# Cross-attention plus FFN on one core: a deeper pipeline, with probabilities and normalised rows turned by DMA transposes instead of TensorE

## The reference, cut to what matters

```python
x = x + _L0_xattn_ref(_layernorm(x, axis=-1), ctx_1024, Wq, Wk, Wv, Wskip)
x = x + _L0_ffn_ref(_layernorm(x, axis=-1), qweight, scales, zeros, bias)

def _L0_xattn_ref(pcd_up, pcd_down, Wq, Wk, Wv, Wskip):
    q = jnp.einsum('oc,bcn->bon', Wq, pcd_up)
    k = jnp.einsum('oc,bcm->bom', Wk, pcd_down)
    v = jnp.einsum('oc,bcm->bom', Wv, pcd_down)
    energy = jnp.einsum('bcn,bcm->bnm', q, k) / jnp.sqrt(C)
    attention = jax.nn.softmax(energy, axis=-1)
    x = jnp.einsum('bnm,bcm->bcn', attention, v)
    return jnp.einsum('oc,bcn->bon', Wskip, pcd_up) + x

def _L0_ffn_ref(x, qweight, scales, zeros, bias):
    w_int = nibbles of qweight, rows interleaved
    w = (w_int - jnp.round(zeros / scales).T) * scales.T
    return jnp.einsum('bsi,io->bso', x, w) + bias
```

## Time and profile before

| | us |
|---|---|
| median of 3 runs | 616.23 |
| the profiled execution, its own time | 616.67 |
| its span in the profile | 614.8 |
| PE busy | 588.1 (96%) |
| DVE busy | 476.5 (77%) |
| POOL busy | 468.7 (76%) |
| ACT busy | 409.4 (67%) |
| granted TensorE clock, mean | 0.989 |

### The profile page before, as it was taken

How to read it: one execution, slowest core, us unless ns; L and a number is a source line. 1 busy time by engine, 2 the same in 40 slices (tenths; PEclk the granted TensorE clock), 3 DMA queues, 4 the chain that set the end, 5 groups by cost and what they waited for, 6 DMA issues and landing times.

```text
span 614.8 us, 10932 instructions
## 1 busy us (share of the span) xinstructions
PE 588.1 (96%) x3348; PEld 416.1 (68%) x3348; DVE 476.5 (77%) x1027; ACT 409.4 (67%) x976; POOL 468.7 (76%) x520
## 2 busy tenths in 40 slices
PE   2868999999999999999999999999999999999996
PEld 2755777667777766777776677777677777667763
DVE  6787877878887777888778788878777877887762
ACT  4874677666668766666876666686666677666650
POOL 2453788777879877777977787897778789777866
PEclk9977999999999999999999999999999999999999
DMA  8011012222111222211222211122221112221002
GB/s 315 3 43 43 27 53 79 77 77 73 40 53 66 77 77 77 70 41 47 73 77 77 77 65 46 43 77 77 77 77 54 57 43 77 77 77 68 19 19 102
DMA packets 20178, 41.38 MB, mean 67 GB/s; under 512 B 2496, under 2 KB 7104, under 8 KB 20160
## 3 DMA queue, kind: packets, MB, share of 16 engines
q1 hardware_dynamic: 19584, 41.03, 19.7%
q10 hardware_dynamic: 576, 0.14, 0.1%
HBM read 24.39 MB, written 16.78 MB: 67 GB/s over the span
## 4 chain that ended last, share of the span: by engine, by line
PE 91%; DVE 5%; ACT 2%; issue 1%; DMA 1%; POOLq 0%; POOL 0%; ACTq 0%
PE ps_y L676 36%; PE ps_e L610 17%; PE ps_o L644 14%; PE ps_t L625 9%; PE ps_o L637 7%; PE ps_t L657 5%; PE ps_kv L688 2%; PE ps_kv L686 2%; DMA sb_x<-in_x_dram 1%; DVE sb_nib L457 1%; ACT sb_prob L288 1%; DVE sb_pt_lo L408 1%; DVE sb_neg_max L398 0%; ACT sb_pt_hi L297 0%; DVE sb_zp L499 0%
## 5 line engine op out<-in xcount | busy, mean ns | idle before, releaser
L288 ACT ACTIVATE sb_prob<-ps_e,sb_neg_max 128x256 f32<-128x256 f32 x256 | 118.7, 470 | 128.9 <-DVE sb_neg_max L398 128.8
L676 PE MATMUL ps_y<-sb_wf,sb_xnt_hi 128*128 128x512 f16 x512 | 196.1, 383 | 0.9 <-DVE sb_xnt_lo L448 0.9
L676 PE MATMUL ps_y<-sb_wf,sb_xnt_lo 128*128 128x512 f16 x512 | 194.0, 379 | 0.0
L214 POOL TENSOR_SCALAR sb_prob<-sb_prob,sb_rsum 128x256 f32<-128x256 f32 x256 | 117.7, 477 | 27.5 <-DVE sb_rsum L403 27.5
L408 DVE TENSOR_TENSOR sb_pt_lo<-ps_t,sb_pt_hi 128x512 fp32r<-128x512 f32 x128 | 88.3, 691 | 34.6 <-ACT sb_pt_hi L297 30.4
L398 DVE TENSOR_REDUCE sb_neg_max<-ps_e 128x2 f32<-128x512 f32 x128 | 87.7, 686 | 34.8 <-PE ps_e L610 34.8
L610 PE MATMUL ps_e<-sb_kv_hi,sb_xc_hi 128*128 128x256 f32 x256 | 91.6, 358 | 7.7 <-DVE sb_kv_lo L535 4.0
L297 ACT ACTIVATE sb_pt_hi<-ps_t 128x512 fp32r<-128x512 f32 x128 | 76.3, 598 | 33.9 <-PE ps_t L625 33.9
L676 PEld LDWEIGHTS ps_y<-sb_wf,sb_xnt_hi 128*128 128x128 f16 x512 | 49.7, 97 | 59.2 <-issue 17.6
L223 POOL TENSOR_TENSOR sb_rstd<-sb_ve,sb_neg_half 128x1 f32<-128x1 f32 x32 | 17.5, 548 | 92.3 <-DVE sb_ve L443 92.3
L250 POOL TENSOR_TENSOR sb_xc_lo<-sb_xc,sb_xc_hi 128x1024 fp32r<-128x1024 f32 x32 | 76.5, 2390 | 9.2 <-ACT sb_xc_hi L343 7.5
(11 more groups left out here) (85 smaller groups left out, 1162.9 us busy)
## 6 DMA issues: line engine op xcount, KB each, us to landing
sb_x<-in_x_dram SPq DMA_DIRECT2D x32, 512.0 KB, 3.3
out_dram<-sb_o SPq DMA_DIRECT2D x64, 256.0 KB, 2.1
...
sb_q<-in_L_ffn_qweight_dram SPq DMA_DIRECT2D x4, 512.0 KB, 6.4
sb_scale_row<-in_L_ffn_scales_dram SPq DMA_DIRECT2D x1, 512.0 KB, 8.7
sb_bias_row<-in_L_ffn_bias_dram SPq DMA_DIRECT2D x1, 512.0 KB, 9.5
...
```

The costliest lines, as they stand in the source:

```text
L214: last = pool.tensor_scalar(prob[:, j, t, :], prob[:, j, t, :], rsum[:, j, t:t + 1], 1.0, ALU.mult, ALU.mult)
L288: done = act.activation(prob[:, j, t, :], ps_e[j % 2][:, t, :], ACT.Exp, bias=neg_max[:, j, t:t + 1], accum_out=esum[:, j, t:t + 1])
L676: last = pe.matmul(ps_y[h][:, :], xnt_p[s][:, kt, :], wf[:, kt, h * HALF:(h + 1) * HALF], start=kt == 0 and s == 0, stop=kt == KT - 1 and ...
```

## The change

All names below are of the kernel after; its line numbers stand in the rows of instructions further down.

- **Transposes leave PE.** ACT rounds the normalised probabilities of a half (128 x 1024) to float16 `p_hi`, DVE makes the float16 rest `p_lo`, and SP issues a DMA transpose for each, SBUF to SBUF (`turn_probs`). The normalised rows are treated alike (`xn_hi` on ACT, `xn_lo` on POOL, `turn_xn`). That is 6 DMA transposes of 128 x 1024 float16 for each item, all on SP's queue, in SP's program order.
- **float16 attention.** The values are float16 in two parts too, scaled by the item's largest context entry: DVE takes it per row (`context_max`), a one-column fp32 matmul against ones sums it over rows into `ps_m`, and four small DVE instructions make the scales (`value_scale`). `residual` multiplies by `o_scale`.
- **Bias and zero point enter through PE.** One more float32r matmul of 512 columns for each FFN half (`seed_l` x `seed_row`); its left side is the row sum in two parts, brought into a row by three small DMAs. The ACT product and the two POOL sums for `rest` go; POOL adds `x1` directly.
- **One step deeper.** Attention of item `t-1`, FFN of `t-2` in step `t`, with three or four buffers for `x`, `xc`, the values, `x1`, and two for the turned rows. `ps_o` is two banks, one for each half.
- **Order.** PE in a step: scores 0, keys and values of `t+1`, attention half 0, scores 1, attention half 1, FFN half 0, scores 2, scores 3, FFN half 1.
- **No loop.** Every step is written out on every engine.
- **Start.** Wv and Wskip are scaled by DVE before they are turned; the zero-point chain is longer (`seed_sources`) and stands behind `value_scale(0)` and `stats1(1)`; `nibbles` and `unpack` are cut into other pieces.

```diff
+            def turn_probs(b, h):
+                sp.wait_ge(phi_done[h], b + 1)
+                if ran(b, 1):
+                    sp.wait_ge(attn_done[h], b)
+                sp.dma_start_transpose(pt_hi[:, h, :, :].rearrange("m k (t n) -> m (k t) n", n=P),
+                                       p_hi[:, h, :, :].rearrange("n k m -> n (k m)")).then_inc(pt_loaded[h], 16)
+                sp.wait_ge(plo_done[h], b + 1)
+                sp.dma_start_transpose(pt_lo[:, h, :, :].rearrange("m k (t n) -> m (k t) n", n=P),
+                                       p_lo[:, h, :, :].rearrange("n k m -> n (k m)")).then_inc(pt_loaded[h], 16)
+            def turn_xn(a):
+                par = a % 2
+                sp.wait_ge(xnhi_done, a + 1)
+                if ran(a, 2):
+                    sp.wait_ge(y_done[1], a - 1)
+                sp.dma_start_transpose(xnt_hi[:, par, :, :],
+                                       xn_hi[:, :, :].rearrange("c k r -> c (k r)")).then_inc(xnt_loaded[par], 16)
+                sp.wait_ge(rs3_done, a + 1)
+                if a == 0:
+                    sp.wait_ge(seed_made, 3)
+                for k, row in ((0, 0), (1, 1), (0, 32)):
+                    sp.dma_start(seed_l[row:row + 1, par, :].bitcast(F32),
+                                 rs3[:, par, k:k + 1].bitcast(F32)).then_inc(rs_loaded[par], 16)
+                sp.wait_ge(xnlo_done, a + 1)
+                sp.dma_start_transpose(xnt_lo[:, par, :, :],
+                                       xn_lo[:, :, :].rearrange("c k r -> c (k r)")).then_inc(xnt_loaded[par], 16)
...
+            def xn_low(a):
+                pool.wait_ge(xnhi_done, a + 1)
+                for k in (0, KT // 2):
+                    last = pool.tensor_tensor(xn_lo[:, k:k + KT // 2, :], xn[:, k:k + KT // 2, :],
+                                              xn_hi[:, k:k + KT // 2, :], ALU.subtract)
+                last.then_inc(xnlo_done, 1)
+
+            def step(t):
+                m, n, b, a, c = t + 2, t + 1, t, t - 1, t - 3
+                if ran(c):
+                    write_out(c, 0)
+                    write_out(c, 1)
+                if ran(b):
+                    normalise(b, 0)
+                if ran(m):
+                    inverse_std1(m)
+                if ran(n):
+                    centred_lo(n, 0)
+                if ran(b):
+                    normalise(b, 1)
+                if ran(a):
+                    inverse_std2(a)
+                if ran(n):
+                    centred_lo(n, 1)
+                if ran(a):
+                    split_row_sum(a)
+                if ran(b):
+                    normalise(b, 2)
+                    normalise(b, 3)
+                if ran(a):
...
+            def probs_hi(b, h):
+                act.wait_ge(norm_done[2 * h], b + 1)
+                act.wait_ge(norm_done[2 * h + 1], b + 1)
+                if ran(b, 1):
+                    act.wait_ge(pt_loaded[h], 32 * b)
+                act.activation(p_hi[:, h, :, :].rearrange("n k (t m) -> n k t m", m=P),
+                               prob[:, 2 * h:2 * h + 2, :, :].rearrange("n j t (k m) -> n k (j t) m", m=P),
+                               ACT.Copy).then_inc(phi_done[h], 1)
...
+            def xn_high(a):
+                act.wait_ge(xn_done, a + 1)
+                if ran(a, 1):
+                    act.wait_ge(xnt_loaded[(a - 1) % 2], nth(a - 1, 2, 32))
+                act.activation(xn_hi[:, :, :], xn[:, :, :], ACT.Copy).then_inc(xnhi_done, 1)
...
+            def step(t):
+                n, b, a = t + 1, t, t - 1
+                if ran(n):
+                    centre(n)
+                if ran(b):
+                    exps(b, 0)
+                if ran(n):
+                    keys_values_hi(n)
+                    centred_hi(n)
+                if t == -1:
+                    unpack(0)
+                if ran(b):
+                    exps(b, 1)
+                if t == 0:
+                    unpack(1)
+                if ran(b):
+                    probs_hi(b, 0)
+                if ran(a):
+                    apply_norm2(a)
+                if ran(b):
+                    exps(b, 2)
+                    exps(b, 3)
+                if t == 0:
+                    unpack(2)
+                if ran(a):
+                    xn_high(a)
...
+            def probs_lo(b, h):
+                dve.wait_ge(phi_done[h], b + 1)
+                dve.tensor_tensor(p_lo[:, h, :, :].rearrange("n k (t m) -> n k t m", m=P),
+                                  prob[:, 2 * h:2 * h + 2, :, :].rearrange("n j t (k m) -> n k (j t) m", m=P),
+                                  p_hi[:, h, :, :].rearrange("n k (t m) -> n k t m", m=P),
+                                  ALU.subtract).then_inc(plo_done[h], 1)
...
+            def step(t):
+                m, n, b, a, q, c = t + 2, t + 1, t, t - 1, t - 2, t - 3
+                if ran(c):
+                    scale_product(c, 1)
+                if ran(b):
+                    row_max(b, 0)
+                if t == -2:
+                    stats1(0, 0)
+                    stats1(0, 1)
+                    aggregate1(0)
+                    variance1(0)
+                    context_max(0)
+                    scale_weights()
+                if ran(n):
+                    value_scale(n)
+                if ran(m) and t > -2:
+                    stats1(m, 0)
+                    stats1(m, 1)
+                    aggregate1(m)
+                if ran(b):
+                    invert(b, 0)
+                if ran(m) and t > -2:
+                    variance1(m)
+                if ran(a):
+                    residual(a, 0)
+                if ran(b):
+                    row_max(b, 1)
+                if ran(a):
+                    stats2(a, 0)
+                if ran(b):
+                    invert(b, 1)
+                if ran(a):
+                    residual(a, 1)
+                    stats2(a, 1)
+                    aggregate2(a)
+                if t == -1:
+                    zero_point_quotient()
+                    zero_point_factor()
+                    seed_sources()
+                if ran(n):
+                    keys_values_lo(n)
+                if t == -1:
+                    nibbles(0)
+                    nibbles(1)
+                if ran(b):
+                    probs_lo(b, 0)
+                    row_max(b, 2)
+                    row_max(b, 3)
+                if ran(m) and t > -2:
+                    context_max(m)
+                if ran(b):
+                    invert(b, 2)
+                if t == 0:
+                    nibbles(2)
+                    seed_rows()
+                if ran(q):
+                    scale_product(q, 0)
+                if ran(b):
+                    invert(b, 3)
+                    probs_lo(b, 1)
+                if t == 0:
+                    nibbles(3)
+
+            run_steps(step)
+
...
+            def skip_attend(a, h):
+                cols = slice(h * HALF, (h + 1) * HALF)
+                if ran(a, 1):
+                    pe.wait_ge(x1_done[h], a)
+                for i, (s, m) in enumerate(HI_LO):
+                    pe.matmul(ps_o[h][:, :], wsk_p[s][:, a % 3, :], xc_p[m][:, a % 3, cols], start=i == 0, stop=False)
+                pe.wait_ge(pt_loaded[h], 32 * (a + 1))
+                for k in range(MT):
+                    for i, (s, m) in enumerate(HI_LO):
+                        last = pe.matmul(ps_o[h][:, :], v_p[s][:, a % 3, k * P:(k + 1) * P], pt_p[m][:, h, k, :],
+                                         start=False, stop=k == MT - 1 and i == 2)
+                last.then_inc(attn_done[h], 1)
+
+            def ffn(q, h):
+                par = q % 2
+                if h == 0:
+                    pe.wait_ge(xnt_loaded[par], nth(q, 2, 32))
+                if ran(q, 1):
+                    pe.wait_ge(prod_done[h], q)
+                else:
+                    pe.wait_ge(rows_done, 2)
+                for kt in range(KT):
+                    if q == 0 and h == 0 and kt % 2 == 0:
+                        pe.wait_ge(wf_done, kt // 2 + 1)
+                    for s in range(2):
+                        pe.matmul(ps_y[h][:, :], xnt_p[s][:, par, kt, :], wf[:, kt, h * HALF:(h + 1) * HALF],
+                                  start=kt == 0 and s == 0, stop=False)
+                if h == 0:
+                    pe.wait_ge(rs_loaded[par], nth(q, 2, 48))
+                pe.matmul(ps_y[h][:, :], seed_l[:, par, :], seed_row[:, h * HALF:(h + 1) * HALF],
...
+            def step(t):
+                n, b, a, q = t + 1, t, t - 1, t - 2
+                if t == -1:
+                    pe.wait_ge(proj_kept, 3)
+                if ran(b):
+                    pe.wait_ge(kvlo_done, b + 1)
+                    pe.wait_ge(xclo_done, b + 1)
+                    scores(b, 0)
+                if ran(n):
+                    keys_values(n)
+                if ran(a):
+                    skip_attend(a, 0)
+                if ran(b):
```

(16 more changed lines are left out.)

697 lines of the change are left out of this document (285 added, 412 removed).

## The result

The kernel after takes 727.66 us (median of 4 runs, 723.48 to 731.81) where the kernel before takes 616.39 (median of 4 runs): 1.181 times the time, 95% interval 1.174 to 1.188. The prediction was 583, and its range ended at 665.

The account below looks back on a forecast made before the run. The prediction took PE to bound the kernel before and DVE with its waits (16.4 us a step) the kernel after: 58 us of start, 492 for 30 steps, 31 of end and 1.9 around gave 583 us, range 560 to 665.

Parts of the forecast that it names:

- What bounds the kernel before: Whole kernel before: PE, busy for 96% of the span, sets the 18.0 us step; DVE and POOL come next.
- PE's step after (15.85 us): PE: 18.01 us less transposes, slower attention and a wait, plus seed and one-column matmuls, gives 15.85 us a step.
- I take the lower end, 256 KB being the size of the store: SP's queue: a transpose holds it only as long as a plain issue, 0.35 us; the upper end was 3.2.
- d: SP's queue: the time for which one DMA transpose holds it, taken at 0.35 us.
- 13.7 + 3d: Round over `p_lo`, SP's transposes, row sums, `xn_lo`'s landing, FFN half and chunk 2: 14.8 us at d = 0.35, hidden.
- DVE's 16.4: DVE's loop with its waits for ACT and POOL: 16.4 us a round, said to set the step.
- rival 1: SP's queue binds a little, d from 0.9 to 1.24: 16.4 to 17.4 us a step, 583 to 616 us; chance 0.18.
- DVE's step of 13.5: DVE's own work a step: 14.4 less 4.4 us removed plus 3.5 added, 13.5 us, not binding alone.
- POOL "shrinks" from 14.6: POOL's work a step: loses two sums of 128 x 1024, gains one and trifles, so falls below 14.6 us.
- Start and end of 89 us: Outside the 30 full steps: 58 us up to the first full step and 31 us behind the last.
- Rival 2: SP's queue becomes the bound, d above 1.24, PE waiting before the first FFN half: slower than 616 us; chance 0.22.
- Rival 3: SP's queue: each transpose issued block by block, d = 2.8, step 22.1 us, kernel 760 us; chance 0.10.

Follow-up runs that it names:

- experiment 9: Kernel after, all engines reordered to give every transposition time, POOL's chunk 1 product before the variance power, DVE's context maximum earlier; 589.27 us, 0.957 times before.
- Experiment 2: Kernel after with only the three row-sum DMAs moved behind the transpose of `xn_lo` on SP; 637.20 us, 1.031 times before.
- Experiment 1: Kernel after with `xn`'s parts made earlier on ACT and POOL and turned ahead of half 1's probabilities on SP; 638.11 us, 1.034 times before.
- experiment 4: Kernel after with each probability transpose cut into two of four blocks, 10 transposes a step instead of 6; 805.5 us in one execution.
- experiment 8: Experiment 1 with row sums last and PE's first FFN half moved ahead of attention half 1; 648.13 us, 1.051 times before.

## Why the prediction was wrong, step by step

- **What bounds the kernel before, and PE's step after (15.85 us)**: right. The step of 19.71 us at full clock holds waits of 0.95 and 3.06, which leaves PE 15.70. In experiment 9 a step of 17.01 us (306.71 to 323.72) holds 1.46 of waiting, which leaves 15.55. The removed and added terms are right in their sum; no run shows them one by one.
- **"I take the lower end, 256 KB being the size of the store"**: this is the step that failed. The price of a transpose was bounded by d = 0.35 and 3.2, and taken at 0.35 because the bytes were those of a store. Measured in the round: mostly 1.23 to 1.33 us of hold. The 0.35 itself was the issue of a load; in the kernel after a store holds the queue for 0.53. The relation "lands 1.75 + d after its issue" came out well for `xn_lo`: 1.75 + 1.3 = 3.05, measured 3.14. With d = 1.3 the prediction's own formula, 13.7 + 3d, gives 17.6, already past DVE's 16.4.
- **The other 3.7 us of the step from 299.19** are three terms of the same sum, mis-sized: the row sums at 3 x 0.35 = 1.05, measured 2.25 from the first issue to the transpose behind them (+1.2); `p_lo` at 1.27, measured 2.15 beside POOL (+0.9); and PE's FFN half at full clock, measured at half for 7 matmuls (+1.4). 17.6 + 1.2 + 0.9 + 1.4 = 21.1, measured 21.27. With the 1.92 that the row sums take in most steps it is 17.6 + 0.9 + 0.9 = 19.4 without the clock, and the steps at full clock take 19.6 to 19.9. Experiment 2 shows the first of them by itself: 3.0 us a step come back for 1.9 to 2.25 of queue.
- **"The queue has nothing else to do for most of a step"**, said against rival 1: true and beside the point. SP's queue isn't busy, but its order puts `xn_lo`, which is ready at 300.3, behind `p_lo` of half 1 and the row sums. Experiment 1 takes both away, experiment 2 the row sums alone, and each brings 90 us.
- **DVE's step of 13.5**: 14.07 measured in the window, 26.24 / 2 = 13.1 in experiment 9, where nothing collides. That DVE and its waits would set the step (16.4) was wrong for the kernel after. It holds for experiment 9, where a round through DVE, POOL and ACT sets 16.84. But that is another order, and its round goes on over `nb`, `xn` and `xn_lo`, which the predicted one did not; that the numbers are so close is in part luck, and 589 is no success of the 583.
- **POOL "shrinks" from 14.6**: it did not, 14.64 in the window, because its sums and DVE's low parts collide. In experiment 9 it is 25.89 / 2 = 12.9.
- **Start and end of 89 us**: 92. First scores were said to come at 21 to 24 us; they come at 25.02.
- **Rival 2 was right**, its place (PE in front of the first FFN half), its mechanism and its sign. Its size was too small: 19.1 us even at its example of d = 1.8, and 17.6 at the d measured, since it knew nothing of the other three terms. It had a chance of 0.22, and nothing in the trace of before spoke against it, for that shows no transpose at all.
- **Rival 3** (block by block) is out: experiment 4 has the same hold for four blocks as for eight. Its 760 us is nearer to 728 than the forecast, but by a mechanism that isn't there. The estimate of over 60 us a step, worked out from the Trainium skill, "VectorE: DVE Perf Modes", section "The three transpose paths", falls with it: eight blocks land in 3.2 to 3.7 us, not in 10.5.
- The Trainium skill, "Advanced Engine Details and Errata", section "X-Bar Transpose (TRN2)", has transposes as fast as regular DMAs. By this trace they are not: a store of the same 256 KB holds SP's queue for some 0.5 us and lands in 2.4, a transpose 1.25 and 3.3. In the order of the kernel after that difference is on the path; in that of experiment 9 it isn't.

What the runs don't settle: what in the two engines' instructions makes them collide, and what makes the clock fall behind one wait and not behind another. In the kernel after it was at the lower level behind waits of 3.21 and 3.03 us and not behind one of 3.08; in experiment 8 it fell 1.4 us after a wait of 1.91 had ended (299.53), and in experiment 9 it stayed up behind 1.46.
